# Routed experts of a graph layer: 64-token column pairs and a conditional second half replaced by one pass of 128 stationary tokens

## The reference, cut to what matters

```python
shared = sum(silu(x @ sWg[e]) * (x @ sWu[e]) @ sWd[e] for e in range(2))
probs = softmax(x @ Wr)                      # 625 x 64
top_w, top_i = top_k(probs, 6)               # six experts for each of the 625 tokens
gate = zeros(625, 64); gate[token, top_i] = top_w / sum(top_w)
for e in range(64):
    routed += (silu(x @ Wg[e]) * (x @ Wu[e])) @ Wd[e] * gate[:, e:e+1]
out = shared + routed + x                    # Wg, Wu, Wd: 64 x 512 x 512 each
```

## Time and profile before

| | |
|---|---|
| median of 3 executions | 995.87 us (992.62 to 999.44) |
| the profiled execution | 995.54 us |
| its span | 993.6 us |
| mean granted TensorE clock | 0.947 |
| TensorE busy | 855.6 us, 86% |
| weight loads busy | 551.1 us, 55% |
| VectorE, ScalarE, GpSimd busy | 547.5, 255.4, 286.5 us |
| DMA read and written | 290.26 MB and 26.62 MB |

### The profile page before, as it was taken

The page is one execution under the profiler, slowest core; times in us unless marked ns, Lnnn a source line. Parts: engine busy times, 40 slices in busy tenths (PEclk is TensorE's granted clock), DMA queues, the critical chain, the costliest instruction groups (busy, mean ns, idle before and its releaser), DMA issues. The chain is left out here.

```text
span 993.6 us, 21562 instructions
## 1 busy us (share of the span) xinstructions
PE 855.6 (86%) x7785; PEld 551.1 (55%) x7785; DVE 547.5 (55%) x1625; ACT 255.4 (26%) x573; POOL 286.5 (29%) x271
## 2 busy tenths in 40 slices
PE   2488887977685789999999989999999999999990
PEld 1243454534342776666565666667666666656660
DVE  7998999999889873333232423333324333333216
ACT  2112111211401222232222222332233222223230
POOL 5675443433001012222222222223222222222111
PEclk9689999988888799999999999999999999999996
DMA  8765687656489706989889999999987999999976
GB/s 277 259 190 192 214 267 228 204 187 194 153 229 396 290 17 242 343 345 387 330 290 359 369 402 408 378 356 404 383 321 294 401 401 380 377 371 375 400 269 229
DMA packets 76935, 300.76 MB, mean 303 GB/s; under 512 B 13730, under 2 KB 14119, under 8 KB 58548
## 3 DMA queue, kind: packets, MB, share of 16 engines
q1 hardware_dynamic: 57256, 254.21, 67.6%
q0 software_dynamic: 17280, 38.48, 12.1%
q10 hardware_dynamic: 2252, 6.06, 1.7%
HBM read 290.26 MB, written 26.62 MB: 319 GB/s over the span
## 5 line engine op out<-in xcount | busy, mean ns | idle before, releaser
L1236 DVE TENSOR_TENSOR arena<-arena 128x288 f32 (+1 forms) x640 | 235.1, 441 | 14.0 <-POOL spare L715 4.4
L1871 PE MATMUL bank<-arena,low 128*64 128x256 f32 x2048 | 240.7, 383 | 1.4 <-issue 1.4
L1871 PEld LDWEIGHTS bank<-arena,low 128*64 128x64 f32 x2048 | 139.9, 137 | 75.1 <-issue 12.8
L1712 PE MATMUL bank<-arena,multi 128*32 128x256 f32 x1584 | 119.7, 436 | 59.9 <-DVE arena L1236 59.8
L1896 PE MATMUL bank<-arena,low 128*64 128x256 f32 x1392 | 161.3, 379 | 1.1 <-ACT low L993 1.1
L756 POOL DMA_INDIRECT low<-xr_d,idx x64 | 90.4, 1412 | 240.7 <-DVE place L1467 178.2
L760 POOL DMA_INDIRECT y_d<-low,place x64 | 68.0, 1062 | 262.1 <-ACT low L1000 181.4
L1896 PEld LDWEIGHTS bank<-arena,low 128*64 128x64 f32 x1392 | 101.4, 137 | 50.2 <-ACT low L993 1.3
L1712 PEld LDWEIGHTS bank<-arena,multi 128*32 128x32 f32 x1584 | 60.1, 124 | 114.5 <-issue 48.4
L693 POOL DMA_INDIRECT arena<-xn_d,ssel x79 | 107.9, 1366 | 36.7 <-issue 21.8
L1000 ACT ACTIVATE low<-bank,gcol 64x256 f32<-64x256 f32 x174 | 81.8, 470 | 105.7 <-PE bank L1896 104.6
(11 more groups left out here) (220 smaller groups left out, 718.3 us busy)
## 6 DMA issues: line engine op xcount, KB each, us to landing
arena<-in_L_ffn_Wg_dram SPq DMA_DIRECT2D x64, 1024.0 KB, 9.2
arena<-in_L_ffn_Wu_dram SPq DMA_DIRECT2D x64, 1024.0 KB, 11.5
arena<-in_L_ffn_Wd_dram SPq DMA_DIRECT2D x64, 1024.0 KB, 8.9
arena<-in_edge_attr_dram SPq DMA_DIRECT2D x88, 256.0 KB, 4.6
arena<-y_d SPq DMA_DIRECT2D x5, 1250.0 KB, 6.4
sums_d<-arena ACTq DMA_DIRECT2D x18, 256.0 KB
arena<-sums_d SPq DMA_DIRECT2D x4, 896.0 KB
arena<-in_L_mix_W_qkv_dram SPq DMA_DIRECT2D x2, 1024.0 KB, 18.8
```

The costliest lines, as they stand in the source:

```text
L1236: return dve.tensor_tensor(prod[:, buf, 0:n, EXT * p:EXT * p + EXT], x1[b][:, 0:n, bass.ds(i1, EXT)], x2[b][:, 0:n, bass.ds(i2, EXT)], ALU ...
L1712: ins = pe.matmul(bank[2 * b + c // 2][at:at + 32, 256 * (c % 2):256 * (c % 2) + 256], pair[:, pairs, i, 32 * s:32 * s + 32], prod[:, buf, ...
L1871: ins = pe.matmul(out_bank[64 * h:64 * h + 64, w * HF:(w + 1) * HF], xgT[:, b, k, 64 * o:64 * o + 64], gu[:, slot, w, k, h * HF:(h + 1) * HF],
```

## The change

All 128 gathered rows become the stationary operand, in one pass for every expert, however many of them are in use. Gate, up and down are four matmuls each of 128 stationary rows and 512 moving weight columns. Gate has a bank for each parity (3, 4) and a semaphore `s_G` of its own, up has bank 6. The conditions, their registers and the second half of an expert go. h is 512 columns wide, so it takes four transposes, and they stand between gate and up of the next expert. Silu starts at the end of gate. `load_down` reads its rows in another order (four neighbouring rows for each partition). The overflow beyond 128 tokens, which was there before and doesn't run on this data, keeps its form.

```diff
-CAP = 64
+CAP = 128
...
             def load_down(slot, w):
-                sp.dma_start(dn[:, slot].rearrange("p (h c) n -> p h c n", h=2),
-                             w.rearrange("(h p c) n -> p h c n", h=2, c=2)).then_inc(s_wd[slot], 16)
+                sp.dma_start(dn[:, slot], w.rearrange("(p c) n -> p c n", c=DC)).then_inc(s_wd[slot], 16)
...
                 if i < NX:
-                    sp.wait_ge(s_xgTp, e + 3)
+                    sp.wait_ge(s_G, e + 1)
                     load_gate(i % GU_RING, wg[i])
+                    sp.wait_ge(s_U, e + 1)
                     load_up(i % GU_RING, wu[i])
...
+            def hT_copy():
+                return act.copy(hT, bank[TURN_BANK][:, :].rearrange("p (c n) -> p c n", c=DC))
+
+            def silu(b):
+                return act.activation(sg, bank[GATE_BANK[b]][:, :], ACT.Silu)
+
+            def scale(i, b):
+                return act.activation(yy[:, b, :], bank[5][:, :], ACT.Copy, scale=gcol[:, i:i + 1])
...
+                if e < NX:
+                    act.wait_ge(s_G, e + 1)
+                    if e >= 1:
+                        act.wait_ge(s_h, e)
+                    silu(e % 2).then_inc(s_sg, 1)
                 if e >= 1:
-                    ov = act.snap(over[(e - 1) % 16], min_val=0, max_val=NX)
                     act.wait_ge(s_hTp, e)
-                    hT_copy(0, bank[2]).then_inc(s_hT, 1)
-                if e < NX:
-                    act.wait_ge(s_U, e + 1)
-                    silu(0, bank[GU_BANK[e % 2]]).then_inc(s_sg, 1)
-                if e >= 1:
+                    hT_copy().then_inc(s_hT, 1)
...
-            def mult(o, in_bank):
-                return dve.tensor_tensor(hh[:, o, :].rearrange("p (c j) -> p j c", c=2), sg[:, o, :].rearrange("p (j c) -> p j c", c=2),
-                                         in_bank[:, HF:2 * HF].rearrange("p (j c) -> p j c", c=2), ALU.mult)
+            def mult():
+                return dve.tensor_tensor(hh.rearrange("p (c j) -> p j c", c=DC), sg.rearrange("p (j c) -> p j c", c=DC),
+                                         bank[UP_BANK][:, :].rearrange("p (j c) -> p j c", c=DC), ALU.mult)
...
                 dve.wait_ge(s_sg, e + 1)
-                mult(0, bank[GU_BANK[e % 2]]).then_inc(s_h, 1)
-                ov = dve.snap(over[e % 16], min_val=0, max_val=NX)
-                with dve.If(0 < ov):
...
+                dve.wait_ge(s_U, e + 1)
+                mult().then_inc(s_h, 1)
...
-            def h_transpose(o, out_bank):
-                for c in range(2):
-                    ins = pe.transpose(out_bank[:, c * 128:(c + 1) * 128], hh[:, o, c * 128:(c + 1) * 128], ident[:, :])
+            def gate_or_up(b, slot, w, out_bank):
+                for k in range(DC):
+                    ins = pe.matmul(out_bank[:, :], xgT[:, b, k, :], gu[:, slot, w, k, :], start=(k == 0), stop=(k == DC - 1))
                 return ins
 
-            def gate_or_up(o, b, slot, w, out_bank):
+            def h_transpose():
+                for c in range(DC):
+                    ins = pe.transpose(bank[TURN_BANK][:, c * 128:(c + 1) * 128], hh[:, c * 128:(c + 1) * 128], ident[:, :])
+                return ins
+
+            def down(slot):
                 for k in range(DC):
...
+                    ins = pe.matmul(bank[5][:, :], hT[:, k, :], dn[:, slot, k, :], start=(k == 0), stop=(k == DC - 1))
                 return ins
...
-                if e >= 1:
-                    ov = pe.snap(over[(e - 1) % 16], min_val=0, max_val=NX)
-                    pe.wait_ge(s_h, e)
-                    h_transpose(0, bank[2]).then_inc(s_hTp, 1)
                 if e < NX:
                     pe.wait_ge(s_xgT, e + 1)
-                    if e < 3:
+                    if e < 2:
                         pe.wait_ge(s_shh, WINDOW - 2 + e)
-                    if e == 0:
-                        pe.matmul(bank[OV][:, HF:2 * HF], ident[:, :], iota[:, 0:HF], start=True, stop=True)
                     pe.wait_ge(s_wg[slot], 16 * fill)
-                    gate_or_up(0, e % 2, slot, 0, bank[GU_BANK[e % 2]])
+                    gate_or_up(e % 2, slot, 0, bank[GATE_BANK[e % 2]]).then_inc(s_G, 1)
                 if e >= 1:
-                    with pe.If(0 < ov):
-                        hold(pe, "pe", o_h, ov & UPTO)
-                        part_transpose(bank[OV]).then_inc(o_hTp, 1)
+                    if e == 1:
+                        pe.wait_ge(s_flags, 1)
+                    pe.wait_ge(s_h, e)
+                    h_transpose().then_inc(s_hTp, 1)
                 if e < NX:
                     pe.wait_ge(s_wu[slot], 16 * fill)
-                    gate_or_up(0, e % 2, slot, 1, bank[GU_BANK[e % 2]]).then_inc(s_U, 1)
...
+                    gate_or_up(e % 2, slot, 1, bank[UP_BANK]).then_inc(s_U, 1)
                 if e >= 1:
                     pe.wait_ge(s_wd[last], 16 * last_fill)
-                    with pe.If(0 < ov):
-                        hold(pe, "pe", o_hT, ov & UPTO)
-                        down(1, last, bank[OV]).then_inc(o_y, 1)
                     pe.wait_ge(s_hT, e)
+                    if e == 1:
+                        pe.wait_ge(s_shh, WINDOW)
                     if e >= 2:
                         pe.wait_ge(s_ys, e - 1)
-                    down(0, last, bank[5]).then_inc(s_y, 1)
-                if e < NX:
...
-                    with pe.If(0 < w2):
-                        hold(pe, "pe", o_ys, w & UPTO)
-                        gate_and_up_part(1, e % 2, slot, bank[OV])
-                    with pe.If(0 < w):
-                        hold(pe, "pe", o_ys, w & UPTO)
-                        gate_and_up_part(0, e % 2, slot, bank[OV]).then_inc(o_U, 1)
+                    down(last).then_inc(s_y, 1)
```

More of the change, by code:

```diff
@@ L412, in gps_layer @@
         s_xgT = sem("s_xgT")
+        s_G = sem("s_G")
         s_U = sem("s_U")
@@ L1506, in add_term @@
                 dve.tensor_tensor(total, total, terms[i], ALU.add).then_inc(s_added, 1)
-            GU_BANK, OV = (3, 4), 6
-            over = offs[0:2 * PLACES]
             for e in range(NX):
-                if e % PLACES == 0:
-                    dve.load(over[e % 16:e % 16 + PLACES], vrow[:, e:e + PLACES])
                 i = e + LEAD
@@ L1574, in _ @@
                         hold(dve, "dve", s_sg, u + NX + 1)
-                        mult(0, bank[GU_BANK[0]])
-                        mult(1, bank[GU_BANK[1]]).then_inc(s_h, 1)
+                        hold(dve, "dve", s_U, u + NX + 1)
+                        mult().then_inc(s_h, 1)
                 for i in range(TOPK - 1):
@@ L1861, in xg_transpose @@
                 return ins
-            def h_transpose(o, out_bank):
-                for c in range(2):
-                    ins = pe.transpose(out_bank[:, c * 128:(c + 1) * 128], hh[:, o, c * 128:(c + 1) * 128], ident[:, :])
-                return ins
-            def gate_or_up(o, b, slot, w, out_bank):
-                for k in range(DC):
-                    for h in range(2):
-                        ins = pe.matmul(out_bank[64 * h:64 * h + 64, w * HF:(w + 1) * HF], xgT[:, b, k, 64 * o:64 * o + 64],
-                                        gu[:, slot, w, k, h * HF:(h + 1) * HF],
-                                        start=(w == 0 and k == 0), stop=(k == DC - 1), skip_group_check=True)
-                return ins
@@ L1876, in gate_and_up_part @@
-            def gate_and_up_part(q, b, slot, out_bank):
-                for k in range(DC):
-                    for w in range(2):
-                        for h in range(2):
-                            at = 64 * w + PART * h
-                            ins = pe.matmul(out_bank[at:at + PART, q * HF:(q + 1) * HF], xgT[:, b, k, CAP + PART * q:CAP + PART * (q + 1)],
-                                            gu[:, slot, w, k, h * HF:(h + 1) * HF], start=(k == 0), stop=(k == DC - 1), skip_group_check=True)
-                return ins
@@ L1920, in _ @@
                 lookup(e % 2, rtab[:, e]).then_inc(s_look, 1)
-            GU_BANK, OV = (3, 4), 6
-            over = [pe.alloc_register(f"pe_over{i}") for i in range(2 * PLACES)]
-            over2 = [pe.alloc_register(f"pe_over2_{i}") for i in range(2 * PLACES)]
             pe.wait_ge(s_xg[0], 16)
@@ L1995, in _ @@
                         hold(pe, "pe", s_xgT, u + NX + 1)
[L1996 to L2000 removed]
+                        hold(pe, "pe", c_w, (u + 1) * 48)
+                        gate_or_up(0, 0, 0, bank[GATE_BANK[0]]).then_inc(s_G, 1)
+                        gate_or_up(0, 0, 1, bank[UP_BANK]).then_inc(s_U, 1)
                         hold(pe, "pe", s_h, u + NX + 1)
[L2002 to L2003 removed]
+                        h_transpose().then_inc(s_hTp, 1)
                         hold(pe, "pe", s_hT, u + NX + 1)
[L2005 to L2006 removed]
+                        down(0).then_inc(c_y, 1)
             pe.matmul(bank[0][0:1, 0:1], ident[:, 0:1], ident[:, 0:1], start=True, stop=True)
```

140 lines of the change are left out of this document (28 added, 112 removed).

## The result

| | before | after |
|---|---|---|
| median of four executions | 994.25 us (990.40 to 999.44) | 1196.06 us (1194.97 to 1197.72) |
| the profiled execution, its span | 995.54, 993.6 us | 1196.89, 1195.1 us |
| the loop, first transposes of x to the end of the last `down` | 370.01 to 971.82: 601.8 us | 369.23 to 1177.70: 808.5 us |
| behind the last `down`, to the end of the span | 21.8 us | 17.4 us |

The ratio is 1.2027 (95% interval 1.1967 to 1.2088); in a second measurement on one chip with five rounds it was 1.2041 (1.2011 to 1.2072). The forecast was 20 us too high on a change of 201.

The account below looks back on a forecast made before the run. TensorE bounds the loop, with DMA close behind. The loop at 824.1 us adds 222.1, the end takes off 2.0: +220.1 on 995.5 gives 1215.6, taken as 1217 us with the closing error; range 1205 to 1231.

Parts of the forecast that it names:

- The overflow's 104.5 us of steps: TensorE's loop: work for experts with more than 64 tokens, 50.6 + 53.9 us, goes with its conditions.
- the idle time: TensorE's loop: of 11.4 us idle, 9.8 was late weights and would go; the other 1.6 stays.
- The wider product, silu and the copies: VectorE and ScalarE in the loop: product 1.1 to 1.2 us, silu and copy 586 ns each, all hidden behind TensorE.
- a full-width group at 3.52 us: Gate, up and down each cost 3.52 us, bounds 3.49 and 3.54, read from shared_down; 10.56 us an expert.
- The shared units, taken over at 82.0: Shared up and down units in the loop keep their old price: 16 x 2.92 + 10 x 3.53 = 82.0 us.
- The end: Behind the last down: shorter scaling and scatters further apart give -2 us, bounds -5 and 0.
- closing error of the steps: Loop steps sum within 0.5% of busy time; pointing upwards (+3 of 590), this took 1215.6 to 1217 us.
- My signs of being wrong: Groups below 3.4 or above 3.6 us, TensorE idle for VectorE or ScalarE, or loop clock below 1.00.
- Overlap of full-width groups: Rival: successive full-width groups in the loop overlap at 1.83 us each; kernel 893, or about 950 with DMA limits; 2%.
- a stall in each expert: Rival: late products and copies, or up's bank freed late, cost 38 to 77 us over the loop, 1255 to 1294; 5%.
- the lower clock: Rival: granted clock falls to 1.2 GHz for a tenth of the loop, +82 us, some 1300; 3%.
- Rival 2: Weights set the loop's pace, so TensorE's work is free and the time stays at 996 us; 2%.

Follow-up runs that it names:

- experiment 1: Changed kernel with its down group alone put back into column tiles, two of 64 rows side by side: 1217.37 us, ratio 1.2232 to the kernel before.
- experiment 2: Changed kernel with gate, up and down all in column tiles of 64 rows: 1228.98 us, ratio 1.2356 to the kernel before.
- experiment 4: Changed kernel with the lookup moved ahead of the transposes of x, so gate follows transposes: 1193.50 us against 1196.67 for the changed kernel.
- experiment 7: Kernel before with longer down-weight runs and interleaved gate/up columns: 1.0097; instead with gate/up loads requested one place later: 0.9987; the latter plus 8 part transposes moved: 0.9959.
- experiment 5: Changed kernel with the scatter of expert 62 held until expert 63's result is there: 1201.53 us against 1196.67 for the changed kernel on one chip.
- experiment 6: Kernel before with its overflow conditions never true, leaving out experts' tokens from 64 on: ratio 0.9526 to the kernel before.

## Why the prediction failed by 20 us, and what in it held

**What held.** TensorE bounds the loop; half the array's partner tiles were doing useful work, and the change serialises their columns. The step from 5.33 us of gate, up and down to over 10 is measured at 3.51 + 3.44 + 3.43 = 10.38. The overflow's 104.5 us of steps go, and with them nearly all of the idle time: one wait of 0.9 us is left in the loop. The wider product, silu and the copies are hidden, and the clock stays at 1.00.

**The term that was mis-sized: a full-width group at 3.52 us.** The 192 groups took 664.6 us, 3.46 on average; 192 x 3.52 is 675.8. That is 11.2 us. The shared units, taken over at 82.0, took 79.4: 2.6 more. My step was to read the price of a group off `shared_down`, see that a change of form costs the transposes 0.05 us, and take at most that off; 3.49 was my lower bound, and up and down came in at 3.44 and 3.43. In the kernel before every full-width unit stands directly behind tiled groups, and experiments 1 and 2 show that it pays 0.10 for that: the same unit takes 2.81 or 2.92, 3.44 or 3.53, by its neighbour alone. The transposes' 0.05 was the smallest of these prices, and I took it for all of them. Gate came in at 3.51, near my 3.52, by luck: what stands ahead of it is the lookup (experiment 4), and no tiled group. Counting 26 units at the old price was the same error once more. The other 1.8 us of the loop are the waits (0.9 where I kept 1.6), and transposes and lookups that the last experts don't have.

A tiled group costs the one ahead of it too (0.09, experiment 1). This bears on a rule of the Trainium skill, TensorEngine Tiling (Array Packing), section Tiling Modes: a change of the tiling mode, unlike a change of tile, drains TensorE. The runs agree in kind, with 0.30 us for the pair of changes of experiment 1. The drain itself was not seen, only its price.

The 131 ns for 512 columns in a sustained stream, which the prediction weighed from the Trainium skill, TensorE: Matmul & The Clock Gate, section Back-to-back issue gap, find no support in this float32 stream after either: the records start every 3.43/8 = 0.43 us. No run here has such a stream in another type.

**A term that was right for a wrong reason: the idle time.** I took 9.8 of the 11.4 idle us as late weights, by the DMA share of the stretches they stand in, and let them go because an expert has 12.9 us for its weights after. They went, but that was luck: no weight was late (experiment 7). They were one late gather and four waits whose cause is open, and the time between the weights, which my argument used, had no part in it that the rows show. A high DMA share beside an idle stretch doesn't show that a load ended it; the landing of that load does.

**The end: -2 us forecast, -4.4 measured.** The chain of the changed kernel, as the earlier trace rows:

```profile
1179.50 5.04 DMA y_d<-low,place
...
1184.97 5.28 DMA arena<-y_d
```

The last scatter lands at 1184.54, 6.8 us behind the last `down`; before at 982.99, 11.2 us behind. The landing is not set by the distance of the two scatters, as I had it: in experiment 5 they are as close as before and the last lands in 2.6 us. The loads of the terms (start of the first and the last in these rows, kernel before, then after) tell more.

```profile
L605 SPq DMA_DIRECT2D arena<-y_d x5: 319/320/434, 951.9 to 975.5; - x5
```

```profile
L593 SPq DMA_DIRECT2D arena<-y_d x5: 319/320/1872, 1145.6 to 1178.5; - x5
```

The load of term 4 waits for the scatter of expert 62. It was issued 3.7 us behind the last `down` (975.5 against 971.82) and is now at 0.8 (1178.5 against 1177.70), 2.9 earlier. Of that, 1.7 is the longer `down` of expert 63: the scatter of 62 begins 3.2 us ahead of its end (1174.47) where it began 1.5 ahead (970.27). The other 1.2 is that the load follows the start of this scatter after 4.1 us and no longer after 5.2. The last scatter lands with it or just behind it: 7.5 us after that issue before, 6.0 after. Before, the load of term 3 (971.06 to 976.94) was on the way too; after, it had landed at 1171.82. That this makes the 1.5 us is not shown by a run. 2.9 + 1.5 = 4.4. Experiment 5 holds this chain up and has an end 4.9 us longer, with a scatter that lands sooner.

**The rest.** The loop begins 0.8 us earlier, 0.65 of it because the gather that its first transposes wait for landed sooner (a wait of 1.11 us for 1.76); I had no term for that. The preparing matmul (0.6 us) stood inside the loop and in none of my sums, so its going adds nothing here. And I had added 1.4 us for a closing error of the steps; there was none to add. In all 15.6 (loop) + 2.4 (end) + 0.8 + 1.4 = 20.2 of the 20.1 us between 1217 and the profiled 1196.9.

**The range.** It was worked out from bounds that hung on one row's reading: -6 us for the group, where -11 came, and the units had no bound at all. The two errors in the loop were of one sign because they had one cause, the neighbours. My signs of being wrong were looser than my range: groups of 3.43 to 3.51 lie within the 3.4 to 3.6 that I had allowed, yet 192 times the difference takes the sum out of it.

**The rivals.** Overlap of full-width groups and a stall in each expert did not occur, nor the lower clock. Rival 2 had a true core: experiment 6 puts the floor of the loads near 560 us, close under the kernel before, but of no concern to a loop that needs 808.

## What to carry to other kernels

A float32 group on TensorE costs the columns that move, whatever rows are in use: where at most 64 rows are needed, put the two halves of the weight columns side by side on the array, and pay for more rows only where they exist. That holds here for 64 against 128 rows and 512 columns. Read the price of a group where its neighbours have the same form as in the changed kernel; if the trace has it only between groups of another form, the bound must take off a change on both sides. Taking work off TensorE pays only down to the floor of the loads, here an estimated 42 us of 602. And before a wait is put down to a load, look up when that load landed.

## What had not been expected of the hardware

- A pair of changes between column-tiled and full-width matmuls costs 0.30 us in experiment 1, spread over the group ahead (0.09), the tiled group (0.15) and the one behind (0.06 to 0.10); the four changes of experiment 2 cost 0.49. Four transposes between two tiled groups take 0.59 us for 0.44.
- A moving operand read as pairs of neighbouring float32 columns, every second pair, is slower: 3.68 us for 3.50 in the same 32 records.
- A gate group behind a 0.13 us lookup takes 3.51 us, behind transposes 3.44.
- The last scatter of 128 rows took 9.3 us from its start to its landing with the loads of two terms (1.25 MB each) on the way, 5.0 with one, and at most 2.6 in experiment 5, where the load was issued 1.4 us behind its start. Part of that is GpSimd's own record, 3.19, 2.97 and 0.98 us. Only the timing of the scatter was changed, not the loads alone.
- Four waits of TensorE in the kernel before, 7.2 us together, end on no semaphore that the trace shows; waits of 0.4 to 2.0 us stand at the same places in the three versions of experiment 7.
